# Other positions in a hand-placed schedule, and 25 instead of 26 products on GpSimd

## What is computed

```python
xi, res = split(x @ W_in.T + b_in)                 # 512 channels each
xi = silu(conv4(xi) + b_conv)
proj = xi @ W_x.T + b_x
delta, B, C = softplus(proj[:512]), proj[512:528], proj[528:]
h_t = exp(delta_t * A) * h_{t-1} + delta_t * B_t * xi_t   # 512 x 16 states, over 1024 steps
y_t = sum_n(h_t * C_t) + xi_t * D
x1 = layernorm(x + (y * silu(res)) @ W_out.T + b_out)
gf = global_net(mean_t(x1)); out = x1
for _ in range(3):
    tf = coupling_net(out)                         # 4 small layers, gelu and sigmoid
    out = out + coupling(gf, tf) * twist(out)      # twist swaps feature quarters and signs
result = layernorm(x1 + out)
```

## Time and profile before

| | us |
|---|---|
| median of 3 runs | 4040.12 (4036.9 to 4040.94) |
| the profiled execution | 4040.28 |
| its span | 4038.5 |
| POOL busy in the span | 3644.6 (90%) |
| PE busy | 3524.4 (87%) |
| DVE busy | 3429.6 (85%) |
| ACT busy | 2959.0 (73%) |
| first L1060 starts at | 60.40 |

### The profile page before, as it was taken

The page is one execution under the profiler, slowest core; times in us unless marked ns, Lnnn a source line. Parts: engine busy times, 40 slices in busy tenths (PEclk is TensorE's granted clock), DMA queues, the critical chain, the costliest instruction groups (busy, mean ns, idle before and its releaser), DMA issues. The chain is left out here.

```text
span 4038.5 us, 51729 instructions
## 1 busy us (share of the span) xinstructions
PE 3524.4 (87%) x18776; PEld 1611.5 (40%) x18776; DVE 3429.6 (85%) x2508; ACT 2959.0 (73%) x3918; POOL 3644.6 (90%) x1604
## 2 busy tenths in 40 slices
PE   7669989899998998989898998989989898897766
PEld 3224353443434344353443434344353443434233
DVE  4988988889898898989889898898989889898861
ACT  4447868778786877868777786877868777785753
POOL 4999999999999999999999999999999999999860
PEclk9779999999999999999999999999999999998888
DMA  5354373543536354373644546454363544546320
GB/s 182 130 175 154 128 230 120 188 152 130 186 130 224 129 191 138 122 229 120 197 148 155 159 152 200 140 187 129 133 218 123 194 149 158 160 138 199 127 86 31
DMA packets 329645, 630.04 MB, mean 156 GB/s; under 512 B 27952, under 2 KB 226608, under 8 KB 329136
## 3 DMA queue, kind: packets, MB, share of 16 engines
q1 hardware_dynamic: 329392, 626.74, 47.0%
HBM read 456.76 MB, written 169.87 MB: 155 GB/s over the span
## 5 line engine op out<-in xcount | busy, mean ns | idle before, releaser
L1060 POOL TENSOR_TENSOR work<-u_q,b_quad 128x1024 f32<-128x1024 f32 x1024 | 2397.3, 2372 | 138.2 <-DMA u_q<-u_scratch 97.1
L816 ACT ACTIVATE da<-delta_q,neg_a 128x1024 f32<-128x1024 f32 x1024 | 1126.3, 1112 | 600.9 <-DVE work L995 430.8
L987 DVE TENSOR_TENSOR_SCAN da<-da,work 128x1024 f32<-128x1024 f32 x608 | 1389.9, 2286 | 151.4 <-ACT da L816 119.7
L1067 POOL TENSOR_TENSOR work<-work,c_quad 128x1024 f32<-128x1024 f32 x416 | 985.2, 2368 | 11.6 <-DVE work L987 11.3
L987 DVE TENSOR_TENSOR_SCAN work<-da,work 128x1024 f32<-128x1024 f32 x416 | 945.9, 2278 | 29.9 <-ACT da L816 28.1
L727 PE MATMUL y_sum<-work,v_all 128*32 128x256 f32 x8192 | 613.3, 399 | 303.3 <-POOL work L1067 190.7
L995 DVE TENSOR_TENSOR work<-da,c_quad 128x1024 f32<-128x1024 f32 x608 | 743.9, 1224 | 28.6 <-DMA c_quad<-bc_scratch 4.6
L752 ACT ACT_TABLE_LOAD x563 | 722.3, 1283 | 14.5 <-DMA v_all<-in_vectors 3.9
L727 PEld LDWEIGHTS y_sum<-work,v_all 128*32 128x32 f32 x8192 | 199.8, 110 | 771.0 <-issue 259.3
L613 PE MATMUL banks<-xi,w_all 128*128 128x512 f32 x1024 | 479.8, 612 | 9.4 <-ACT g_act L797 5.1
L600 PE MATMUL banks<-xi,taps 128*128 128x512 f32 x984 | 453.2, 606 | 0.0
(11 more groups left out here) (86 smaller groups left out, 3270.3 us busy)
## 6 DMA issues: line engine op xcount, KB each, us to landing
delta_q<-delta_scratch SPq DMA_DIRECT2D x256, 512.0 KB, 5.8
u_q<-u_scratch SPq DMA_DIRECT2D x256, 512.0 KB, 6.1
delta_scratch<-delta SPq DMA_DIRECT2D x64, 512.0 KB, 2.9
u_scratch<-soft SPq DMA_DIRECT2D x64, 512.0 KB, 2.9
b_quad<-bc_scratch SPq DMA_DIRECT2D x64, 512.0 KB, 4.7
c_quad<-bc_scratch SPq DMA_DIRECT2D x64, 512.0 KB, 7.1
s_quad<-res_scratch SPq DMA_DIRECT2D x128, 256.0 KB, 4.1
y_scratch<-s_quad SPq DMA_DIRECT2D x128, 256.0 KB, 3.2
```

Of the source, the lines that this page charges most:

```text
L816: act.activation(da[:, t % 2, :], delta_q[:, slot, :], ACT.Exp, scale=neg_a[:, t % PERIOD:t % PERIOD + 1]).then_inc(da_ready, 1)
L987: dve.tensor_tensor_scan(dst, da[:, t % 2, :], work[:, slot, :], 0.0, ALU.mult, ALU.add) \
L1060: pool.tensor_tensor(work[:, slot, :], u_q[:, copied, :], b_quad[:, j, :], ALU.mult) \
L1067: pool.tensor_tensor(work[:, un % WORK, :], work[:, un % WORK, :], c_quad[:, un % PHASE, :], ALU.mult) \
```

## The change

Only numbers in the tables change. GpSimd gets 25 of the 64 products of a period instead of 26, and mostly others than before; VectorE gets 39 instead of 38. Side work moves by at most one or two units on PE, ACT, DVE; the issue of transfers moves by up to 20 units.

```diff
-POOL_AT = (1, 4, 6, 8, 9, 10, 11, 12, 16, 18, 21, 24, 28, 32, 33, 36, 42, 44, 49, 52, 55, 56, 58, 59, 60, 61)
+POOL_AT = (0, 4, 5, 8, 9, 11, 16, 17, 22, 25, 26, 28, 32, 33, 41, 42, 46, 49, 52, 55, 56, 58, 59, 60, 61)
-X_AT = (0, 0, 19, 24, 37, 37, 45, 49)
-V_AT = (2, 3, 27, 29, 41, 41, 53, 52)
-RES_AT = (0, 1, 26, 26, 36, 39, 47, 50)
+X_AT = (0, 1, 19, 24, 36, 37, 45, 49)
+V_AT = (2, 3, 28, 28, 41, 41, 53, 52)
+RES_AT = (0, 0, 24, 26, 36, 39, 47, 50)
-T_AT = (15, 15, 15, 15)
+T_AT = (15, 15, 15, 16)
-F_AT = (-1, 0, 1, 2, 4, 5, 6, 9, 10, 10)
-G_AT = (16, 19, 21)
-E_AT = (57, 58, 59, 61)
+F_AT = (0, 0, 0, 2, 4, 5, 6, 9, 10, 10)
+G_AT = (17, 18, 21)
+E_AT = (57, 58, 60, 61)
-DST_AT, UST_AT = (7, 5, 10, 8), (11, 5, 8, 9)
-DLD_AT, ULD_AT = (12, 13, 18, 19), (12, 13, 17, 20)
-SLD, YST = -1, 0
-YGLD_AT = (2, 4, 4, 8)
-RESST_AT = (4, 28, 47, 61)
-X1ST_AT = (15, 16)
-RES_IN_AT = 28
-XRES_AT = 66
-OUT_AT = (64, 64)
-XFEAT_AT = 48
-BCST_AT = 54
-LB_AT, LC_AT = (59, 55, 57, 63), (61, 62, 61, 63)
-SILU_AT = (8, 32, 45, 55)
+DST_AT, UST_AT = (8, 5, 10, 6), (9, 8, 8, 8)
+DLD_AT, ULD_AT = (11, 12, 17, 17), (11, 15, 17, 20)
+SLD, YST = 3, -1
+YGLD_AT = (1, 3, 3, 10)
+RESST_AT = (9, 30, 46, 59)
+X1ST_AT = (10, 11)
+RES_IN_AT = 48
+XRES_AT = 65
+OUT_AT = (61, 63)
+XFEAT_AT = 49
+BCST_AT = 52
+LB_AT, LC_AT = (55, 53, 60, 59), (60, 61, 61, 63)
+SILU_AT = (7, 32, 45, 55)
```

More of the change, by code:

```diff
@@ L76 @@
 DELTA_TAKE, DELTA_MAX, U_LAG = 3, 3, 6
-O_STATS, O_RS, O_NORM = 3, 5, 4
+O_STATS, O_RS, O_NORM = 3, 5, 3
 T_TAKE = 3
```

## The result

The changed kernel takes 4054.54 us (median of 5 runs), the kernel before 4039.01 us beside it: a ratio of 1.0042, 95% interval 1.003 to 1.0053. It is **slower by 0.4%**, where 1.5% faster was forecast. All comparisons are therefore ratios to the kernel before on the same chip.

What follows compares the result with a forecast made beforehand. POOL, chained with DVE, was taken to bound the kernel, no engine being full. Fourteen periods at −4.3 us, first and last at −2.3, start +3.8: span 3977.5, plus 1.8 around it, 3979 us; range 3942 to 4020.

Steps and rivals of the forecast that it cites:

- What bounds the kernel: Whole period of 241.75 us: 98 POOL instructions at 2.33 plus 13.7 of waits, POOL and DVE forming one chain.
- One product from POOL to DVE: Each period: POOL has one instruction less, −2.33 us; DVE has one product more, +1.3.
- Units 0 to 27: Stretch before POOL's u at position 28: −2.3 us a period, one POOL product, with bounds 0 and −4.9.
- the wait of 3.44 before the gate of unit 8: DVE between units 8 and 9: wait blamed on POOL's late product, expected to go, −3.4 us on DVE.
- the wait at 28: POOL's wait for DVE's delta at u = delta·xi, 4.99 us before: expected to fall below 2.
- its own sum: DVE in units 0 to 27, by the gate: −1.0 us at best, +1.5 at worst; −2.3 was taken at position 28.
- The wait for C at unit 1: DVE's product 1 needs the second part of C, landing at 1500.2 after scan 1 ends at 1499.1: +1.1 us.
- The loads behind the stores of x1: POOL at unit 20: new wait of 4.2 us for u, costing nothing by itself, with 0.8 us of slack at 28.
- Rival D: Slower: the u load behind the second x1 store lands late, at 10 us instead of 6.1; 4059 us, chance 0.10.
- Units 36 and 56, and the start: POOL's waits of 2.90 at 36 and 3.3 at 56: no gain of their own; first unit later once, +3.8 us.
- The change of periods: Between periods, at unit 0 and the B load for unit 3: −2.0 us a period, bounds 0 and −3.4.
- The mark of B: Rival: POOL's waits only move, still summing to 13 or more a period; only its 2.33 is gained; 4007 us, chance 0.19.

Runs made afterwards that it cites:

- the fastest kernel: Both losses taken out: changed kernel with the transfers as before and the gate's second layer at position 19 instead of 18; 4010.07 us, ratio 0.9908 to the kernel before.
- the overlong filling: Changed kernel with 14 extra matmuls a sequence on PE, 8 ahead of its wait for x and 6 ahead of the third transpose; 4180.5 us, ratio 1.036.
- the run with one number back: Changed kernel with the second layer of the coupling's gate at position 19 instead of 18; 4023.61 us, ratio 0.9933 to the kernel before.
- The filling: Changed kernel with three unused matmuls in PE's wait for the x of the residual; 4035.92 us, ratio 0.9971 to the kernel before.

## Why the prediction was wrong, point by point

**What bounds the kernel.** Right as a sum, wrong as a choice of engines. A period is POOL's instructions at 2.32 us plus its waits: 97 × 2.32 + 18.9 = 243.9 for the 244.2 measured, and with 15.1 of waits 240.1 for the fastest kernel's 240.1. But PE was left out of the argument, although DVE's 40.2 us of waiting for PE's sums stood in the earlier trace rows. Of its delays between units 5 and 24 about 8 in 11 us reached the time in the overlong filling, and 1.0 us less of waiting at L653 gave 2.8.

**One product from POOL to DVE.** Right on the work: 1588 POOL instructions in all, and 12.4 us less in six periods. Not on the time: alone, it gave 0.15%, since POOL's waits grew.

**Units 0 to 27: the step that failed.** It took −2.3 at position 28. Four things in it were wrong.

First and above all, it gave the moved side work of this stretch (`T_AT`, `F_AT`, `G_AT`) no price at all, as if one unit up or down could only shift small tasks on an engine with room. By the run with one number back, the gate's second layer alone costs 1.1% (ratio 1.0042 against 0.9933), of the 1.9% between the forecast of 0.985 and the measured 1.0042. The rest was not taken apart; ACT's wait of 1.81 for PE, ahead of DVE's scans of units 20 and after, is another thing that the moved side work brought, its cost not shown.

Second, the wait of 3.44 before the gate of unit 8 was put down to POOL's product, for which PE did wait 1.33 us there before. It became longer instead: 4.78 us in the period shown, since the sum stands on PE behind the output projection, which waits for the x of the residual (L634, 17.5 us in six periods). The filling brought DVE's waits for sums from 44.2 to 35.0. DVE at that gate, kernel after:

```profile
1519.48 0.69 DVE L967 TENSOR_TENSOR s_quad<-y_sum,s_quad 128x512 f32<-128x512 f32 x1 [4.78 <-PE y_sum L727]
```

Third, the wait at 28 was to be taken by POOL's having less to do. It is DVE that ends last there. POOL's wait for delta fell to 1.56, below 2 as the prediction said, and the product just ahead of it waits 4.46 for a scan. The gain was counted at the instruction where the wait stood, not at the event for which it waited. Even in the fastest kernel POOL's waits for DVE are (38.1 + 14.1) / 6 = 8.7 us a period, where before they were 6.0: the 32.4 of the earlier trace rows and 3.5 for products, over six.

Fourth, the forecast left its own sum. For DVE it had −1.0 at best and +1.5 at worst, and it said that POOL waits for DVE at 28; by that, POOL's instruction less could not give −2.3 there.

The wait for C at unit 1, put at 1.1, was 11.7 us in six periods, 2.0 each. (Counted from 1493.6, as the prediction has it, 7.1 more is 1500.7 and not 1500.2, which makes 1.6.)

**The loads behind the stores of x1.** The wait came, 5.3 us at unit 16 and 1.5 at unit 20 instead of 4.2 at 20. That it costs little was right: moving the stores back changed the time by 0.2%, within the intervals. Rival D was therefore not the main cause, although the sign was its sign. Nor does the first store hold the load for unit 16 up: SP issued eleven transfers without a pause from the store of u at 1533.31 on (four for the gate's rows and four y loads among them), and the load's turn came at 1539.69. The second store does hold SP, until 1550.08, waiting for the norm (58.6 us in six periods); the load for unit 20 follows it. SP in order of time, the first store of x1 and a load behind it:

```profile
1538.53 0.43 SPq L495 DMA_DIRECT2D x_scratch<-big  x1
...
1539.69 0.88 SPq L400 DMA_DIRECT2D u_q<-u_scratch  x1
```

Unit 16 starts at 1545.54, 5.85 us after that load's issue, where the median landing was 6.1. The Trainium skill, DMA: Bandwidth & Descriptors, section Queues, rings and completion order, has each DMA engine consume descriptors in ring order; as the prediction read it, the store ahead would have made the load later by its own time, and this row does not show that.

**Units 36 and 56, and the start.** Right: POOL has no wait left at either, and none above 0.4 us from unit 36 to the end of the period. The first unit starts at 63.1 instead of 60.4, +2.7 for +3.8.

**The change of periods.** About right: POOL waits 0.38 at unit 0 (1724.0) instead of 1.83, and 1.2 for B behind it.

**The rivals.** The mark of B, waits that still sum to 13 or more, was met at 18.9, but B had them moved and not grown. B put the time at 4007, 0.992 of before; the kernel with the two losses taken out has 0.991. That fit is in part luck: the new list of products alone gave 0.15% and not 0.9%, and the 0.991 needs the new side work with the gate at 19 and the old transfers. The slow side was held by D alone, a mechanism of DMA; none of the rivals put a loss on PE or ACT. That is what the 0.10 on slower missed, and why the range ended at 4020.

What stays open: what DVE's waits for ACT's da cost (54.7 us in six periods with the gate at 19 against 42.7 before; the longest stand behind ACT's wait of 1.81 for PE), and why the new transfers, alone on the kernel before, cost 2%.

## What to carry to other kernels

A position in a hand-written order has side results: here, which bank a task inherits, and so for whose read it waits. When tasks swap places ahead of a small matmul, work out whose buffer each one gets before and after, and price every wait that this makes, even on an engine that is not the busiest. When a loop's first iterations are as fast as forecast and the later ones are not, look for what differs between them, count all that differs, and put one number back at a time. And try the filling of an idle gap of TensorE with unused matmuls of just its length: two rows then show whether the matmuls behind the gap ran slower for it.

## What was new about the hardware

Idle time of PE can be paid twice, in the wait and in the matmuls behind it. After 2.69 us without work the granted clock over the next 4.1 us was 0.59, and four fp32 matmuls took 3.07 us instead of 1.89; after 2.90 us at L653 two took 3.51 instead of 1.98. Ahead of both waits the clock was 1.00. But the length of a wait alone does not decide it. Of the twelve waits of 2.90 at L653 in the kernel after, eleven were followed by slow matmuls; of the ten waits of 1.90 with the gate at 19, five. Ahead of L634 in the kernel after, waits of 2.45, 3.19 and 3.25 us were followed by full speed, and in the kernel before one of 2.13 us was not. Of the single periods above, those with a mean clock of 0.93 and 0.94 take 246.2 and 244.5 us and PE is busy for 222.3 and 221.3 in them; those at 0.96 and 0.99 take 235.4 and 235.8, with 214.7 and 214.4.

An unused matmul of 128x512 in fp32 is two records. Three in a row took 2.84 us and eight 7.13, 0.95 and 0.89 each, so that a filling must be counted in matmuls of that length.
